# Group norm per batch, a centred x3 and regrouped start-up work in a four-block convolution and attention kernel

## What is computed

```python
# L0: group norm (32 groups of 4 channels), attention over 256 positions
xr = x.reshape(b, 32, 4 * 256)
xn = (xr - mean(xr)) * rsqrt(var(xr) + 1e-6);  hn = xn * gamma + beta
q, k, v = wq @ hn + bq, wk @ hn + bk, wv @ hn + bv
x = wp @ (v @ softmax(q.T @ k / sqrt(128)).T) + bp + x
# L1: position attention, then channel attention;  L2: 8 heads with an added embedding
# L3: linear attention
f = (x - mean_c(x)) * rsqrt(var_c(x) + 1e-5) * norm_g       # chan_ln, over the channels
q, k, v = dwconv3x3(q_w @ f), dwconv3x3(k_w @ f), dwconv3x3(v_w @ f)
...                                                          # softmaxes, context, out_w, two feed-forward products
```

## Time and profile before

| | before |
|---|---|
| median of 3 runs | 83.38 us (83.35 to 83.53) |
| the profiled execution: its time, its span | 83.13 us, 81.3 us |
| busy PE, DVE, ACT, POOL | 72.1, 57.6, 48.6, 29.4 us (89%, 71%, 60%, 36% of the span) |
| chain that ended last, by engine | PE 54%, DVE 29%, ACT 4%, POOL 3%, DMA 3% |
| granted TensorE clock | full in all 40 slices |

### The profile page before, as it was taken

The page is one execution under the profiler, slowest core; times in us unless marked ns, Lnnn a source line. Parts: engine busy times, 40 slices in busy tenths (PEclk is TensorE's granted clock), DMA queues, the critical chain, the costliest instruction groups (busy, mean ns, idle before and its releaser), DMA issues.

```text
span 81.3 us, 1649 instructions
## 1 busy us (share of the span) xinstructions
PE 72.1 (89%) x575; PEld 55.0 (68%) x575; DVE 57.6 (71%) x210; ACT 48.6 (60%) x133; POOL 29.4 (36%) x62
## 2 busy tenths in 40 slices
PE   4995999999999997939898999999999799779960
PEld 1342799857888775727465755999999597646830
DVE  1347887897678639776678343789999868898540
ACT  4300487367842708395967398997996654627430
POOL 7911470005983374000000030099599202155400
PEclk9999999999999999999999999999999999999999
DMA  0899600000000000000000000000000000000003
GB/s 8 220 372 399 249 5 0 0 0 0 8 4 0 4 0 0 0 0 8 0 0 0 8 0 0 0 0 0 8 0 4 0 0 0 4 0 0 0 4 125
DMA packets 1304, 2.91 MB, mean 36 GB/s; under 512 B 144, under 2 KB 784, under 8 KB 1296
## 3 DMA queue, kind: packets, MB, share of 16 engines
q1 hardware_dynamic: 1152, 2.68, 9.4%
q10 hardware_dynamic: 144, 0.13, 0.5%
HBM read 2.55 MB, written 0.26 MB: 35 GB/s over the span
## 4 chain that ended last, share of the span: by engine, by line
PE 54%; DVE 29%; ACT 4%; POOL 3%; DMA 3%; issue 2%; POOLq 0%
DVE kacc L797 6%; DVE nmx L753 6%; PE bank L1117 5%; PE bank L1156 4%; DMA x<-in_x 3%; POOL rs L221 3%; PE bank L1297 3%; PE bank L1143 2%; PE bank L1060 2%; DVE st L531 2%; PE bank L1006 2%; PE bank L978 2%; PE bank L949 2%; PE bank L1043 2%; PE bank L1129 2%; DVE pairmax L747 2%
## 5 line engine op out<-in xcount | busy, mean ns | idle before, releaser
L221 POOL TENSOR_TENSOR rs<-ve,mhalf 128x2 f32<-128x2 f32 x8 | 5.6, 696 | 24.8 <-DVE ve L538 24.7
L378 ACT ACTIVATE pT<-bank 128x512 f32<-128x512 f32 x16 | 8.5, 602 | 1.7 <-PE bank L1143 1.3
L1218 PE MATMUL bank<-convw,fsh 128*128 128x128 f32 x72 | 9.2, 275 | 0.0
L1218 PEld LDWEIGHTS bank<-convw,fsh 128*128 128x128 f32 x72 | 8.7, 193 | 0.1
L753 DVE TENSOR_REDUCE nmx<-bank 128x2 f32<-128x512 f32 x10 | 6.4, 686 | 3.2 <-PE bank L1117 3.2
L271 POOL TENSOR_TENSOR vacc<-vacc,vprod 128x225 f32<-128x225 f32 x8 | 5.1, 636 | 5.1 <-ACT vprod L418 5.1
L240 POOL TENSOR_TENSOR convw<-wgc,tapw 128x128 f32<-128x128 f32 x9 | 3.8, 455 | 7.6 <-DVE wgc L704 7.6
L797 DVE SCALAR_TENSOR_TENSOR kacc<-bank,wc,kacc 128x240 f32<-128x240 f32 (+1 forms) x16 | 6.3, 446 | 0.0
L418 ACT ACTIVATE vprod<-bank,wc 128x256 f32<-128x256 f32 x14 | 5.9, 500 | 0.0
L915 PE MATMUL bank<-warm 128*128 128x512 bf16 x13 | 4.7, 507 | 1.2 <-DVE warm L540 1.2
L1117 PE MATMUL bank<-km,qm 32*128 32x256 f32 x64 | 4.6, 400 | 0.0
(11 more groups left out here) (220 smaller groups left out, 195.0 us busy)
## 6 DMA issues: line engine op xcount, KB each, us to landing
wc<-in_pack_c SPq DMA_DIRECT2D x1, 649.0 KB, 7.0
wb<-in_pack_b SPq DMA_DIRECT2D x1, 612.0 KB, 6.0
tapw<-in_taps SPq DMA_DIRECT2D x1, 576.0 KB, 7.9
wa<-in_pack_a SPq DMA_DIRECT2D x1, 320.0 KB, 3.9
out<-y SPq DMA_DIRECT2D x2, 128.0 KB, 1.7
x<-in_x ACTq DMA_DIRECT2D x1, 128.0 KB, 2.8
x<-in_x SPq DMA_DIRECT2D x1, 128.0 KB, 2.6
wa<-in_pack_a SPq DMA_DIRECT2D x1, 72.5 KB, 2.6
```

The source lines that it names most:

```text
L221: nc.gpsimd.tensor_tensor(dst, src, mhalf[:, 0:width], ALU.pow).then_inc(done, 1)
L378: nc.scalar.activation(pT2[u % PT2_RING][:, :, :], tiles(bank[SCORE_T_BANKS[u % HG]]), ACT.Exp).then_inc(s["e2_d"], 1)
L1218: product = nc.tensor.matmul(LA[b][:, j * C:(j + 1) * C], fsh[dx][b][:, row:row + H // NT, :].rearrange("p h w -> p (h w)"), convw[:, 3 * ...
```

## The change

Five things change; the rest of the diff is bookkeeping of semaphores.

1. **Group norm as a chain for each batch.** DVE does `bn_stats`, `bn_aggr` and the mean square of batch 0, then those of batch 1. PE has one averaging product for each batch. ACT squares the group's mean out of PSUM (`gsq0`), one DVE step makes the variance from PSUM (`ve0`), another mean times gamma (`gm0`). POOL takes one root for each batch. The shift `nb0` is made from `gm0` and no longer needs `a0`.
2. **Warming products** stand as 8, 2 behind the first averaging product, 1 behind the second, and 2 as before.
3. **First weights in two transfers.** `wv0` and `wpT0` come first (`a2_in`, 128 KB), `wqT0`, `wkT0` and `ident` next (`a3_in`, 192 KB). PE waits for `a3_in` ahead of `q0_product`.
4. **x3 centred where it is scaled.** `wg_mean` and `centre_wg` are gone. A new DVE step `x3_shift` makes minus mean times root (`mrs3`), and `f_scale` adds it as a bias: it waits for DVE now, not for POOL.
5. **convw later.** The nine tap products use `wg` and stand on POOL behind `key_steps` of batch 1, no longer ahead of `xb2_sum`.

PE also gets waits that name what it used to rely on through other waits: `xb1_transposes`, `embedding`, `pam_transposes`, `v2_product`, `x3_ident`, `conv`, `ff_mean_1`, `ff_mean_2`, `ff_product`, `v0_product`.

```diff
@@ sync
-            sp.dma_start(wa[:, first:width_a], pack_a[:, first:width_a]).then_inc(s["a2_in"], 16)
+            second = at_a[SECOND_A[-1][0]][1]
+            sp.dma_start(wa[:, first:second], pack_a[:, first:second]).then_inc(s["a2_in"], 16)
+            sp.dma_start(wa[:, second:width_a], pack_a[:, second:width_a]).then_inc(s["a3_in"], 16)
@@ gpsimd
-            pool.wait_ge(s["ve0_d"], 1)
-            nc.gpsimd.tensor_tensor(rstd0[:, :], ve0[:, :], mhalf[:, 0:NB], ALU.pow).then_inc(s["rstd0_d"], 1)
+            for b in range(NB):
+                pool.wait_ge(s["ve0_d"], b + 1)
+                nc.gpsimd.tensor_tensor(rstd0[:, b:b + 1], ve0[:, b:b + 1], mhalf[:, 0:1], ALU.pow).then_inc(s["rstd0_d"], 1)
...
+            def tap_weights(b):
+                pool.wait_ge(s["prep_w"], PREP_WG)
+                pool.wait_ge(s["tap_in"], 16)
+                for t in range(TAPS):
+                    nc.gpsimd.tensor_tensor(convw[:, t, :], wg[:, C:2 * C], tapw[:, t * C:(t + 1) * C], ALU.mult).then_inc(s["conv_w"], 1)
@@ scalar
+            for b in range(NB):
+                act.wait_ge(s["g0_p"], b + 1)
+                nc.scalar.activation(gsq0[:, b:b + 1], bank[4 * b][:, 0:1], ACT.Square).then_inc(s["gsq_d"], 1)
...
-                act.wait_ge(s["rs3_d"], b + 1)
+                act.wait_ge(s["mrs3_d"], b + 1)
                 for t in range(NT):
-                    nc.scalar.activation(fT[b][:, t, :], tiles(LA[b], 4)[:, t, :], ACT.Copy, scale=rs3[b][:, 0, t:t + 1]).then_inc(s["fT_d"], 1)
+                    nc.scalar.activation(fT[b][:, t, :], tiles(LA[b], 4)[:, t, :], ACT.Identity, bias=mrs3[b][:, t:t + 1],
+                                         scale=rs3[b][:, 0, t:t + 1]).then_inc(s["fT_d"], 1)
@@ vector
+            def group_variance(b):
+                dve.wait_ge(s["gsq_d"], b + 1)
+                nc.vector.tensor_scalar(ve0[:, b:b + 1], bank[4 * b][:, 1:2], EPS_GN, gsq0[:, b:b + 1],
+                                        ALU.add, ALU.subtract).then_inc(s["ve0_d"], 1)
+                nc.vector.tensor_scalar_mul(gm0[:, b:b + 1], bank[4 * b][:, 0:1], A("gamma")).then_inc(s["vec"], 1)
...
+            for stage, b in ((group_inputs, 0), (group_inputs, 1), (group_variance, 0), (group_variance, 1),
+                             (group_norm, 0), (group_norm, 1)):
...
+            def x3_shift(b):
+                dve.wait_ge(s["rs3_d"], b + 1)
+                nc.vector.scalar_tensor_tensor(mrs3[b][:, :], mv3[b][:, 0, :, 0], -1.0, rs3[b][:, 0, :], ALU.mult, ALU.mult).then_inc(s["mrs3_d"], 1)
@@ tensor
-            pe.wait_ge(s["gin0_d"], NB)
-            pe.wait_ge(s["a_in"], 16)
-            nc.tensor.matmul(bank[0][:, 0:2 * NB], A("gmean"), mv0[:, :, :].rearrange("p b m -> p (b m)"),
-                             start=True, stop=True).then_inc(s["g0_p"], 1)
-            keep_clock(3, bank[7])
+            for b in range(NB):
+                pe.wait_ge(s["gin0_d"], b + 1)
+                if b == 0:
+                    pe.wait_ge(s["a_in"], 16)
+                nc.tensor.matmul(bank[4 * b][:, 0:2], A("gmean"), mv0[:, b, :], start=True, stop=True).then_inc(s["g0_p"], 1)
+                keep_clock(2 - b, bank[7])
...
-                nc.tensor.matmul(bank[7][:, 0:3 * C], K("cmean"), wg[:, :], start=True, stop=True).then_inc(s["wgm_p"], 1)
...
-                             (x3_stats, 0), (o2_norm_of(0), 1), (o2_norm_of(1), 1), (k_taps(0, 3), 0), (x3_stats, 1),
+                             (x3_stats, 0), (x3_shift, 0), (o2_norm_of(0), 1), (o2_norm_of(1), 1), (k_taps(0, 3), 0), (x3_stats, 1),
```

162 lines of the change are left out of this document (76 added, 86 removed).

## The result

| | before | after |
|---|---|---|
| median of 17 runs each | 83.33 us (83.12 to 83.53) | 83.57 us (83.11 to 83.86) |
| profiled execution: its time, its span | 83.13, 81.3 us | 83.46, 81.7 us |

The ratio is 1.0028 (95% interval 1.0015 to 1.0040): the change made the kernel 0.28% slower. The forecast was 82.77, 0.7% faster, with a range that ended at 83.3. Intervals here leave out runs that lie over 1.5% above a kernel's fastest, among them three lone executions at 140 to 235 us.

The account below looks back on a forecast made before the run. The chain was taken as bound by the group norm until 7.50 us, then PE, then DVE from 54.03 to 63. Terms -0.45 - 0.33 + 0.17 = -0.61 took 83.38 to 82.77 us, range 82.1 to 83.3.

Parts of the forecast that it names:

- +0.17: Path from x3 to f: the added x3_shift step on DVE's chain loses 0.17 us in all.
- would have waited for PE anyway: x3, batch 0: DVE's wait for POOL at x3_shift was said to cost nothing, as DVE waits for PE there.
- PE's stall of 0.48: x3, batch 1: f comes 0.48 us later and PE stalls about that long, covered by its 0.47 wait at 63.83.
- bounds given, 0 to 0.48: x3 loss: 0 if a kc held by POOL swallows the step, 0.48 us if PE's stall goes through.
- rival 4: Path to f costs its full 0.48 or more, kc falling behind another POOL addition (0.69): 83.08 to 83.63 us; chance 0.1.
- -0.45: Group norm chain at the start: the first q product starts at 7.05 rather than 7.50, a gain of 0.45 us.
- the second part land at 5.6: First weights: the a3_in transfer lands at 5.6 us, ahead of the first product, so the split costs nothing.
- rival 1: Group norm: hn0 on DVE is not held by POOL's root of batch 1; -0.77, 82.61 us; chance 0.2.
- end well ahead of 7.05: Warming products on PE before the first q product only fill waits and finish before its 7.05 us start: nothing.
- -0.33: PE around 18 us: removing the mean of the L3 weights gains 0.33 us.
- the second exponential: Batch 0, ending at 19.28 us: what is late next once the L3 mean goes, letting the third transpose start at 19.32.
- rival 3: About 34.2 us: convw on POOL slows DVE's four pair maxima by 0.84; +0.23, 83.61 us; chance 0.06.

Follow-up runs that it names:

- c1_x3_alone: before with only the x3 part (no weight mean, x3_shift, biased scaling; convw and two clears behind the key steps): 83.91 against 83.30 us, ratio 1.0068.
- a6_bias_zero: after without x3_shift, the scaling reading a column of zeros as bias, so x3 stays uncentred: 82.47 us, ratio 0.9897.
- a4_held_b: after with SP waiting for a3_in before issuing pack_b and all behind it: 83.70 us, one run; the 192 KB needed 3.3 us to land.
- d3_shifted: before with group norm chain, regrouped warming products, new waits, and eight one-column clears starting DVE's list: 82.92 against 83.35 us, ratio 0.9957.
- after_again: after unchanged, measured a second time against before: 83.57 against 83.35 us, ratio 1.0026.
- a1_one_transfer: after with the 320 KB of first weights in one transfer: 83.31 against 83.37 us, ratio 1.0005.
- c2_gap13: before with group norm chain, 13 warming products, L3 weights centred by one product in a PE wait, convw and four clears behind key steps: 82.80 us, ratio 0.9930.
- c6_gap15: c2_gap13 with two more warming products behind the rest: 82.76 us, ratio 0.9930.
- b3_gap_fewer: a3_both with 9 warming products and weights centred by one product in a PE wait, copied by ACT: four runs 82.50 to 82.72 us, two 83.76 and 85.13.
- a3_both: after with one transfer of first weights and the old x3: 83.33 us, ratio 0.9989.
- a2_x3_undone: after with the old centring of the weights on PE and DVE and no x3_shift: 83.15 against 83.37 us, ratio 0.9987.

## Why the prediction was wrong, point by point

**x3: the step that failed.** The sum had +0.17; it measured +0.88 in c1_x3_alone and +0.90 in after's profile. Two sentences of the working were wrong.

"For batch 0 DVE ... would have waited for PE anyway." DVE would, but the scaling isn't DVE's. The path is variance, root, scaling on ACT, transposes on PE. The timeline of before, batch 0:

```profile
47.77 0.17 DVE L538 TENSOR_SCALAR ve<-mv 128x2 f32<-128x2 f32 x1
...
48.78 0.62 ACT L394 ACTIVATE fT<-bank,rs 128x128 f32<-128x128 f32 x2
...
50.40 0.70 PE L1227 MATMUL bank<-fsh,wgc 128*128 128x256 f32 x2
```

And of after:

```profile
47.19 0.17 DVE L546 TENSOR_SCALAR ve<-mv 128x2 f32<-128x2 f32 x1
...
48.19 0.16 DVE L789 SCALAR_TENSOR_TENSOR mrs<-mv,rs 128x2 f32<-128x2 f32 x1 [0.84 <-POOL rs L222]
...
48.39 0.81 ACT L401 ACTIVATE fT<-bank,mrs,rs 128x128 f32<-128x128 f32 x2 [0.34 <-DVE mrs L789]
...
49.25 0.14 PEld L1208 LDWEIGHTS bank<-wa,fT 128*128 128x128 f32 x1 [0.20 <-ACT fT L401]
...
50.05 0.70 PE L1238 MATMUL bank<-fsh,wg 128*128 128x256 f32 x2
```

Variance to the next product took 2.63 before and 2.86 after: of the 0.58 us that after was ahead, 0.35 is left, and 0.23 is lost that the sum had at nothing. The pair of scalings went from 0.62 to 0.81, so PE now waits for each of them singly: four times, 1.3 us in all for both batches, where before it waited once, 0.4 us.

For batch 1 the sum said that PE's stall of 0.48 would end in the wait of 0.47 at 63.83. That wait is for `ek` of batch 1, which hangs on `kc`, the end of DVE's own row: a wait that moves along with DVE's chain can't cover a delay in that chain. In after it is still 0.47, at 64.15. What came, from after's timeline:

```profile
54.70 0.36 DVE L789 SCALAR_TENSOR_TENSOR mrs<-mv,rs 128x2 f32<-128x2 f32 x1
...
55.60 0.68 PE L1208 MATMUL bank<-wa,fT 128*128 128x128 f32 x2 [0.27 <-ACT fT L401]
...
56.99 0.42 DVE L817 TENSOR_REDUCE mq<-bank 128x16 f32<-128x256 f32 x1 [0.37 <-PE bank L1229]
```

PE's stall went through to `q_max` (`mq`): its products of the q convolution ended late, and DVE stood 0.37 us for them, where before it followed `kc` at once. The step also took 0.36 and not 0.17. From variance to `mq` the chains have 3.04 before and 3.49 after (+0.45), from there to `kc` 5.32 and 5.54 (+0.22, with `qn` at 0.58 for 0.45). Of the bounds given, 0 to 0.48, even the upper one was too low, since it held one batch only. The doubt stood in rival 4, at 0.1 and up to 83.63, and that time came nearest. Its mechanism didn't: `kc` fell behind no further addition of POOL (0.43 at batch 0, where before had 0.62, and 0.93 at batch 1 in both). Nor does its upper end follow from its terms: -0.45 - 0.33 + 0.48 + 0.69 is +0.39, 83.77 us, and not +0.25.

The scaling itself was costed at its old length. The view of the tile `fT` (min/median/max ns, first and last start) of before and after:

```profile
L394 ACT ACTIVATE fT<-bank,rs x4: 359/408/455, 48.8 to 55.1; 128x128 f32<-128x128 f32 x4
```

```profile
L401 ACT ACTIVATE fT<-bank,mrs,rs x4: 449/454/458, 48.4 to 55.4; 128x128 f32<-128x128 f32 x4
```

With a bias from a tile each of the four takes about 0.45. The two of batch 0 grew by 0.09 (0.367 and 0.359 to 0.458 and 0.449); those of batch 1 took 0.45 before already and 0.45 to 0.46 after, for a reason that no run shows. a6_bias_zero shows what the bias is worth on the path there, 0.22. The Trainium skill ("ScalarE: Activation LUTs", What ACT_TABLE_LOAD costs) has it: each operand of one value per partition adds about 93 ns to an activation. The 90 ns at batch 0 agree, and the prediction could have taken them into its sum.

**First weights: forecast nothing, cost some 0.2 to 0.3, not clear of noise.** The prediction had the second part land at 5.6, "since the bytes ahead of it are the same", and named a landing behind 7.0 as what would make it wrong. It landed at 2.09 + 5.13 = 7.22, within the stated upper bound of 8.1, and held the q product to 7.27, while `hn0` had ended at 6.90. In the other kernels with the split and `pack_b` right behind it landed at 6.4 to 7.35, never near 5.6. The failed step is the sentence on the bytes ahead: a4_held_b, a single run, shows that the bytes behind count. The second wait of PE, some 0.1 us, was not in the sum either.

**Group norm: -0.45 forecast, -0.43 by medians** in d3_shifted, where it stands alone but for the eight clears. That the two agree is luck, since the mechanism behind -0.45 was not there. `hn0` overlapped batch 1's root (6.10 to 6.65) by 0.17 us and took 0.41, as without it, so it wasn't held, and rival 1 was right on that: `hn0` ended at 6.90, and 7.01 was forecast. What took the gain away again was another thing in each execution: the transfer (after), or slow warming products that delay the second averaging product and with it `a0` and `hn0` (after_again). The steps themselves were costed well: `a0` started at 6.06 as forecast, `hn0` at 6.49 for 6.43, and a root of one column took 0.55 where the sum had 0.70. By the Trainium skill ("SBUF — State Buffer", Who interferes with whom), `hn0` would have waited for the whole root if it ran in the two-port mode; its rows here don't show a wait, those on the clears below do.

**Warming products: forecast nothing.** They "end well ahead of 7.05" only where the pace doubles early. after_again shows the other case, with the first q product at 7.56.

**Mean of the L3 weights: -0.33 forecast, -0.35 to -0.39 measured** (stretch of after, c1_x3_alone and a1_one_transfer). The reading of what is late next, the second exponential, was right.

**convw and rival 3.** The pair maxima beside `convw` kept their 0.20 (chain of after):

```profile
34.47 0.20 DVE pairmax L752
```

Missed was what stood behind `convw` on POOL: four clears, which moved forward to 12.33. There they met the centring of `out_w` on DVE. Before, and after with the last clear:

```profile
12.84 0.21 DVE L680 TENSOR_SCALAR outwc<-wc 128x128 f32<-128x128 f32 x1
```

```profile
12.61 0.87 DVE L690 TENSOR_SCALAR outwc<-wc 128x128 f32<-128x128 f32 x1
...
13.09 0.31 POOL L241 MEMSET vodd<- 128x256 f32 x1
```

The step was held until 13.48, 0.08 behind the end of the last of four clears at 13.40. In after it stands in the chain, and PE started the second block's first product 0.10 later behind the first q product than in before (7.88 and 7.78), but by the group scores nothing is left of that (20.74, as c1_x3_alone, which has the clears elsewhere, 20.73). The prediction held the move of `convw` itself free, which it was.

**The sum as it came out**, by medians: group norm -0.43, split +0.26, mean -0.36, x3 +0.88, together +0.35; measured +0.24. The four come from different comparisons, each uncertain by some 0.15, so the difference is not explained further. Of the kernels that compute the same, c2_gap13 and c6_gap15 are 0.7% faster than before: they keep the group norm and the shorter PE row, and leave x3 as it was. The four low runs of b3_gap_fewer lie lower still, but two of its six do not.

**Open.** Why the pace doubles, and the first weights land, at another time in another execution. Whether the split's 0.26 is real, and why the second of two transfers lands later than one transfer of the same bytes. Why a3_both isn't faster than a2_x3_undone. Whether it is the fetch that makes the gap in DVE's list.

## What to carry to other kernels

Before a wait is booked as cover for a delay, ask what ends it: if that is the end of the chain that is delayed, it moves along and covers nothing. A step taken off a busy engine and put, however small, between a root and the engine that waits for it costs its own time, both hand-overs and the wait of each engine behind, in every batch. And a transfer's landing depends on what is issued behind it; here a split that put the urgent part last landed it at 6.4 to 7.35 us, and the whole in one transfer at 5.3 to 6.9.
